# Four 64x64 tiles for a block-of-ones matmul, and an exponential in three parts

## The chip, the cores and the metric

The kernel runs on one core of one Trainium2 chip. The time is that of the device for the whole program, in microseconds: 4799.18 us, the median of three runs (4795.73 to 4809.79).

## The reference

The input is `x` of shape (8, 512, 128), float32. The model has two stages:

```
x = x + attn(layernorm(x))        # 16 heads of 8, causal, weights 1/(lambda - s) with four Newton steps
x = x + ffn(layernorm(x))         # "ffn" is six layers, each: local attention, then a gated MLP
```

One layer of the second stage, for a sequence of 512 tokens and width 128:

```
qkv = shift_tokens(x) @ Wqkv              # 16 heads of 64
q = q / max(norm(q over the head's 64), 1e-12) * q_scale ; the same for k
q, k = rotated (cos, sin, growing and shrinking scale)
attention in windows of 32 tokens, each looking at its own and the window before
x = out @ Wo + x
x = (a * gelu(gate)) @ W2 + b2 + x        # a, gate from layernorm(shift_tokens(x)) @ W1 + b1
```

The change concerns the norms: for every token and head the sum of 64 squares, for q and for k.

## The kernel before, in words

Stage one is untouched. Stage two runs 48 steps, one for each of 6 layers and 8 sequences. In each step the 16 heads are worked in four groups `g` of four heads. Activations lie transposed: partitions are features, columns are the 512 tokens. A projection gives q (or k) of a group as 128 partitions x 2 halves x 512 columns. Partition 32h + i holds feature i of head h, and the second half holds feature 32 + i of the same head.

For one group, the chain is:

- `project` (TensorE) writes q and k into two PSUM banks each.
- `squares` (ScalarE) squares them into `sq`, `rotate` (VectorE) multiplies them by the tables.
- `square_sums` (GpSimd) adds the two halves into `sqs` (128 x 2 x 512, index `which` is 0 for q and 1 for k), `add_rotated` (GpSimd) adds the rotated products.
- `norms` (TensorE) multiplies `sqs` by `ones4`, a 128x128 matrix with ones in its four 32x32 diagonal blocks and zeros elsewhere. So every partition gets its own head's sum. q goes to the first bank, k to the second.
- `log_norms` (ScalarE) takes the logarithm into `lnn`, `inverse_norms` (ScalarE) the exponential of -1/2 of it into `rn`.
- `finish` (VectorE) multiplies `rn` into the rotated q and k.
- `rotated` (SP) sends them with eight DMAs into `qkn`; `scores` (TensorE) reads `qkn`.
- Then `mask`, `row_max` (VectorE), `less_max` (GpSimd), `exponentials` (ScalarE), `denominators` (VectorE), `normalise` (GpSimd), `turn` (TensorE), `turned` (ScalarE), `weigh` (TensorE), `weighted` (VectorE), and for the whole step `out_project`, the layer norm and the MLP.

Every engine has its own `body(b)`, in which the calls for steps b, b-1 and b-2 stand in an order written out by hand. An engine works strictly through this order; semaphores make it wait for others. On TensorE a norms block stands at four places. norm3 (of step b-1) is between `turn` of group 0 and `weigh` of group 0. norm0 is between the two parts of `weigh` of group 1. norm1 is between the first part of `weigh` of group 2 and the first part of `scores` of group 0. norm2 is between the first part of `scores` of group 1 and `values` number 2. PSUM's eight banks are shared by the list `HOLD`; `take` waits until the last holder of a bank was emptied. For instance `mean` takes bank 4 after `values` number 2 (`v2`), which ScalarE copies out.

`scores` and `weigh` already work with small tiles. In `scores` the rows of the array are split in two (the contraction is over 64 partitions) and its columns in four; in `weigh` both are split in two. In both, the two halves of the rows write different PSUM banks. float32 matmuls are recorded as two passes each, with a weight load before each pass.

Of the kernel before, what the change touches and what calls it, by code (L numbers as in the profile page):

```python
# [15 lines left out]
ACT = mybir.ActivationFunctionType  # L16
AX = mybir.AxisListType

P = 128
# [1019 lines left out]
def stage2(nc, consts, wqkv, wod, w1d, w2d, vecd, hist, x1d, out, early):  # L1039
    with ExitStack() as ctx:  # L1040
        def sb(name, shape, dt=F32):
            return ctx.enter_context(nc.sbuf_tensor(name, shape, dt))

        def sem(name):
            return ctx.enter_context(nc.semaphore(name))
# [9 lines left out]
        ones4 = early.ones4  # L1055
# [7 lines left out]
        sqs = sb("sqs", [P, 2, SEQ])  # L1063
        m1 = early.m1
        m2 = early.m2
        lnn = sb("lnn", [P, 2, SEQ])
        rn = sb("rn", [P, 2, SEQ])
# [19 lines left out]
        cst = sb("cst", [P, 4])  # L1087
# [25 lines left out]
        s_rn = sem("s_rn")  # L1113
# [55 lines left out]
        def at(n, k=0, per=NG):  # L1169
            return per * n + (per + k + 1)  # L1170


        def live(b, back):
# [10 lines left out]
        ]  # L1184
        PLACE = {name: i for i, (name, _, _) in enumerate(HOLD)}
        ONE = ("wo", "mean", "var", "gate1", "up1", "out")

# [11 lines left out]


        HELD_LAST = {c: max((back, i) for i, (name, back, _) in enumerate(HOLD) if c in banks(name)) for c in range(8)}
        Y_BANK = [c for c in range(8) if HELD_LAST[c] < (HOLD[PLACE["var"]][1], PLACE["var"])]

# [180 lines left out]
        def _(pe):  # L1384
# [64 lines left out]
            def project(n, g, which, out):  # L1449
# [2 lines left out]
                    mm = pe.matmul(out[:, half, :], wg[:, g, c:c + P], xs[:, 0:SEQ], start=True, stop=True)  # L1452
                mm.then_inc(s_proj[which], 1)

            def norms(n, g, out):
                for which in range(2):
                    mm = pe.matmul(out[:, which, :], ones4[:, :], sqs[:, which, :], start=True, stop=True)  # L1457
                mm.then_inc(s_norm, 1)


# [83 lines left out]
            def body(b):  # L1544
# [30 lines left out]
                if live(b, 1):  # L1575
                    take("norm3", b)
                    squares_due(b - 1, 3)
                    norms(b - 1, 3, bank("norm3"))
# [48 lines left out]
                if live(b, 0):  # L1627
                    take("norm0", b)
                    squares_due(b, 0)
                    norms(b, 0, bank("norm0"))  # L1630
# [29 lines left out]
                if live(b, 0):  # L1660
                    take("norm1", b)
                    squares_due(b, 1)
                    norms(b, 1, bank("norm1"))
# [61 lines left out]
        def _(act):  # L1725
# [12 lines left out]
            def inverse_norms(n, g):  # L1738
                act.wait_ge(s_nf[0], at(n - (g < 1), (g - 1) % NG))
                act.sem_inc(held["act"], 1)  # L1740
                act.wait_ge(s_nf[1], at(n - (g < 1), (g - 1) % NG))
                act.sem_inc(held["act"], 1)
                act.wait_ge(s_lnn, at(n, g))
                nc.scalar.activation(rn[:, :, :], lnn[:, :, :], ACT.Exp, scale=-0.5, bias=cst[:, 2:3]).then_inc(s_rn, 1)

            def values(n, i):
                half, part = i // 2, i % 2
# [47 lines left out]
            def body(b):  # L1795
# [11 lines left out]
                if live(b, 0):  # L1807
                    inverse_norms(b, 0)
# [14 lines left out]
                if live(b, 0):  # L1823
                    inverse_norms(b, 1)
# [10 lines left out]
                if live(b, 0):  # L1835
                    inverse_norms(b, 2)
# [439 lines left out]
```

## Time and profile before

| | |
|---|---|
| median of three runs | 4799.18 us |
| the profiled execution | 4804.87 us |
| its span, first to last instruction | 4803.1 us |
| TensorE (matmul) busy | 4079.8 us, 85% |
| VectorE busy | 3988.7 us, 83% |
| GpSimd busy | 3483.6 us, 73% |
| ScalarE busy | 2994.3 us, 62% |
| norms matmul (line 1457), 768 recorded passes | 383.5 us |
| exponential for `rn` (line 1744), 192 | 1.150 us each |

Shares are averages over both stages; stage two begins at about 1486 us and takes the rest. A matmul's recorded time contains its way through the array, and the next one starts before it ends, so busy times of TensorE overlap. The rows below are of stage two, most of them of one step, and all times in them are in microseconds from the start of the span.

### The profile page before, as it was taken

Reading aid. Unit: us, or ns where it says so; the run is one execution under the profiler, and the core shown is the slowest. Engines: PE = TensorE matmul, PEld = TensorE weight load, DVE = VectorE, ACT = ScalarE, POOL = GpSimd, SP = SyncE. Lnnn points to the kernel's source line nnn. Section 1 sums busy time; section 2 is a strip of 40 time slices with the busy share of each in tenths; the row PEclk is TensorE's granted clock in tenths of the full one; section 3 lists DMA queues with packets and bytes.
Section 4 is the critical chain, followed back from the end, with each engine's and each line's share of the span. In section 5 each row is a group of like instructions: output and inputs, shape, how many; then the busy total and the mean of one; then the engine's idle time right before and its main releaser. Section 6 shows DMA issues by size and latency. Waiting matters only on the chain.

```text
span 4803.1 us, 153853 instructions
## 1 busy us (share of the span) xinstructions
PE 4079.8 (85%) x60260; PEld 2120.9 (44%) x60260; DVE 3988.7 (83%) x7132; ACT 2994.3 (62%) x4240; POOL 3483.6 (73%) x1655
## 2 busy tenths in 40 slices
PE   3666666666656999999999999999999999999997
PEld 1222332233223455555555555555555555555554
DVE  6999999999974788888888888888888888888885
ACT  5999999999983455545555555555555455554552
POOL 4999899999984676667666676666666676666663
PEclk9755555555557999999999999999999999999998
DMA  0000000000003444444444444454444444454443
GB/s 14 3 6 5 10 5 9 5 10 5 3 7 90 103 103 112 118 119 103 105 117 119 114 103 112 118 126 102 103 117 120 114 101 111 118 127 101 104 115 102
DMA packets 230497, 381.82 MB, mean 79 GB/s; under 512 B 38112, under 2 KB 59232, under 8 KB 229728
## 3 DMA queue, kind: packets, MB, share of 16 engines
q1 hardware_dynamic: 229856, 372.57, 32.1%
q8 instruction: 489, 8.01, 0.7%
q14 instruction: 152, 1.25, 0.1%
HBM read 51.57 MB, written 18.61 MB: 15 GB/s over the span
## 4 chain that ended last, share of the span: by engine, by line
PE 46%; issue 6%; DVE 5%; SPq 4%; POOL 3%; DMA 3%; ACT 2%; DVEq 0%; POOLq 0%
PE pb L1452 11%; PE pb L1510 7%; PE pb L1470 6%; PE pb L1493 6%; PE pb L1457 5%; PE pb L1504 4%; PE pb L1521 3%; SPq L1284 3%; PE pb L1533 3%; POOL sqs L1878 3%; DMA qkn<-early 3%; ACT early L1730 2%; PE pb L1480 2%; DVE early L2015 2%; DVE early L1992 1%
## 5 line engine op out<-in xcount | busy, mean ns | idle before, releaser
L783 POOL TENSOR_TENSOR early<-early 128x1280 f32<-128x1280 f32 x416 | 954.9, 2319 | 141.1 <-ACT early L634 139.4
L1878 POOL TENSOR_TENSOR sqs<-early 128x1024 f32<-128x1024 f32 x192 | 468.6, 2441 | 756.5 <-ACT early L1730 756.5
L634 ACT ACTIVATE early<-S,lam 128x512 f32<-128x512 f32 (+3 forms) x2048 | 951.9, 553 | 84.6 <-DVE lam L927 73.2
L1882 POOL TENSOR_TENSOR early<-early 128x1024 f32<-128x1024 f32 x384 | 947.8, 2486 | 19.0 <-DVE early L1992 17.5
L898 DVE BATCH_NORM_STATS2 stats<-early 128x6 f32<-128x512 f32 (+3 forms) x2048 | 832.3, 478 | 57.4 <-POOL early L783 56.2
L1452 PE MATMUL pb<-early 128*128 128x512 f32 x1536 | 734.9, 606 | 2.6 <-POOL early L1955 2.5
L1991 DVE TENSOR_TENSOR early<-pb,early 128x1024 f32<-128x1024 f32 x384 | 467.4, 1217 | 128.1 <-ACT early L1730 115.1
L1730 ACT ACTIVATE early<-pb 128x1024 f32<-128x1024 f32 x384 | 394.0, 1026 | 269.5 <-PE pb L1452 268.9
L2015 DVE SCALAR_TENSOR_TENSOR early<-rn,early 128x1024 f32<-128x1024 f32 x384 | 513.2, 1357 | 54.6 <-POOL early L1882 50.4
L1735 ACT ACTIVATE lnn<-pb,cst 128x1024 f32<-128x1024 f32 x192 | 212.5, 1107 | 492.7 <-PE pb L1457 492.5
L1893 POOL TENSOR_TENSOR pr<-pr,rsum 128x1024 f32<-128x1024 f32 x192 | 365.2, 1902 | 178.7 <-DVE rsum L2028 178.7
L1992 DVE TENSOR_TENSOR early<-pb,early 128x1024 f32<-128x1024 f32 x384 | 465.7, 1213 | 0.0
L1888 POOL TENSOR_TENSOR sm<-sm,mx 128x1024 f32<-128x1024 f32 x192 | 409.2, 2131 | 70.2 <-DVE mx L2006 70.2
L1760 ACT ACTIVATE pr<-sm 128x1024 f32<-128x1024 f32 x192 | 202.2, 1053 | 389.9 <-POOL sm L1888 389.9
L1999 DVE TENSOR_TENSOR sm<-pb,early 128x1024 f32<-128x1024 f32 x192 | 235.0, 1224 | 241.5 <-PE pb L1470 241.4
L1457 PE MATMUL pb<-sqs,early 128*128 128x512 f32 x768 | 383.5, 622 | 32.6 <-POOL sqs L1878 18.6
L1452 PEld LDWEIGHTS pb<-early 128*128 128x128 f32 x1536 | 278.4, 191 | 295.8 <-issue 284.7
L1470 PEld LDWEIGHTS pb<-qkn 64*32 64x32 f32 x24576 | 270.2, 106 | 274.1 <-issue 273.0
L1504 PE MATMUL pb<-early 128*128 128x512 f32 x768 | 367.1, 600 | 1.3 <-ACT lnn L1735 1.3
L1470 PE MATMUL pb<-qkn 64*32 64x64 f32 x24576 | 322.9, 225 | 49.0 <-DVE early L1992 26.1
L423 PE MATMUL psD<-kT,qT 9*128 9x512 f32 (+3 forms) x1024 | 200.3, 741 | 192.5 <-DVE S L889 110.4
L1766 ACT COPY pT<-pb 128x1024 f32<-128x1024 f32 x192 | 194.5, 1013 | 256.9 <-PE pb L1480 256.1
(122 smaller groups left out, 7371.9 us busy)
## 6 DMA issues: line engine op xcount, KB each, us to landing
qkn<-early SPq DMA_DIRECT2D x1536, 128.0 KB, 2.4
vr<-v SPq DMA_DIRECT2D x96, 768.0 KB, 5.8
vr<-v SPq DMA_DIRECT2D x96, 192.0 KB, 5.5
xr<-hist SPq DMA_DIRECT2D x48, 256.0 KB, 4.8
hist<-xo SPq DMA_DIRECT2D x47, 256.0 KB, 4.7
early<-wqkv SPq DMA_DIRECT2D x24, 384.0 KB, 3.5
early<-hist SPq DMA_DIRECT2D x48, 128.0 KB
vr<-v SPq DMA_DIRECT2D x96, 64.0 KB, 6.3
```

Of the source, the lines that this page charges most:

```text
L634: ins = nc.scalar.activation(W[:, p, h, c], S[:, j % 2, h, c], ACT.Abs_reciprocal_sqrt, bias=lam[:, j, i:i + 1])
L783: nc.gpsimd.tensor_tensor(W[:, p, h, :], W[:, p, h, :], W[:, p, h, :], ALU.mult).then_inc(s_wp[p], 1)
L898: ins = nc.vector.bn_stats(out=stats[:, p, h * NBLK + u, :], in_=W[:, p, h, UOFF[u]:UOFF[u] + UNIT[u]])
L1452: mm = pe.matmul(out[:, half, :], wg[:, g, c:c + P], xs[:, 0:SEQ], start=True, stop=True)
L1457: mm = pe.matmul(out[:, which, :], ones4[:, :], sqs[:, which, :], start=True, stop=True)
L1470: mm = pe.matmul(out[o:o + 32, b, (2 * k + s) * 64:(2 * k + s + 1) * 64], qkn[64 * b:64 * b + 64, p, hh, 0, (w + 1) * WIN:(w + 2) * WIN], ...
L1504: mm = pe.matmul(out[:, j, :], xs[:, k * P:(k + 1) * P], wg[:, 2 * half:2 * half + 2, 4 * P:6 * P], start=True, stop=True)
L1730: nc.scalar.activation(sq[:, which, :, :], bank(f"{'qk'[which]}{g}")[:, :, :], ACT.Square)\
L1878: nc.gpsimd.tensor_tensor(sqs[:, :, :], sq[:, :, 0, :], sq[:, :, 1, :], ALU.add).then_inc(s_sqs, 1)
L1882: nc.gpsimd.tensor_tensor(m1[:, which, :, :], m1[:, which, :, :], m2[:, which, ::-1, :], ALU.add)\
L1992: nc.vector.tensor_tensor(m2[:, which, :, :], src[:, :, :], tab[:, which, 1, :, :], ALU.mult)\
L2015: nc.vector.scalar_tensor_tensor(out=nf[:, which, :, :], in0=rn[:, which, :].unsqueeze(1).broadcast_to([P, 2, SEQ]), scalar=1e12, in1=m1[: ...
```

## The change

Each of the two norms matmuls becomes two, of a 64x64 block of `ones4`. The block of ones is block-diagonal, so its off-diagonal 64x64 blocks are zero and are left out. For q the lower half of the partitions goes to the lower half of the output, and the upper to the upper. For k they change places: the lower half of `sqs` is written to partitions 64 to 127 and the upper to 0 to 63. So the four matmuls use the four different 64x64 tiles of the array. q's two write one bank, at different partitions, k's two the other.

`lnn` then holds k's halves swapped. The exponential is done in three instructions: q's whole, and k's two halves, each written to the other half of the partitions.

```diff
             def norms(n, g, out):
                 for which in range(2):
-                    mm = pe.matmul(out[:, which, :], ones4[:, :], sqs[:, which, :], start=True, stop=True)
+                    for half in range(2):
+                        i, o = 64 * half, 64 * (half ^ which)
+                        mm = pe.matmul(out[o:o + 64, which, :], ones4[i:i + 64, i:i + 64], sqs[i:i + 64, which, :],
+                                       start=True, stop=True, tile_position=(i, o))
                 mm.then_inc(s_norm, 1)
...
                 act.wait_ge(s_lnn, at(n, g))
-                nc.scalar.activation(rn[:, :, :], lnn[:, :, :], ACT.Exp, scale=-0.5, bias=cst[:, 2:3]).then_inc(s_rn, 1)
+                nc.scalar.activation(rn[:, 0, :], lnn[:, 0, :], ACT.Exp, scale=-0.5, bias=cst[:, 2:3])
+                nc.scalar.activation(rn[0:64, 1, :], lnn[64:P, 1, :], ACT.Exp, scale=-0.5, bias=cst[64:P, 2:3])
+                nc.scalar.activation(rn[64:P, 1, :], lnn[0:64, 1, :], ACT.Exp, scale=-0.5, bias=cst[0:64, 2:3])\
+                  .then_inc(s_rn, 1)
```

## Rows read from the trace of the kernel before

**Rows 1.** Busy time by engine, 2000:2900: window, length, PE, PEld, DVE, ACT, POOL, clock, DMA share, GB/s.
```profile
2000.00:2900.00 900.00, 869.12 (x15354) 468.27 (x15354) 750.93 (x805) 468.28 (x481) 614.27 (x280) 1.00 0.47 114
```
**Rows 2.** Waits in 2000:2900: waiting line, releaser, total us, times, longest.
```profile
PE pb L1470 <- DMA qkn<-early: 4.4, 12, 0.5
PE pb L1457 <- POOL sqs L1878: 3.5, 14, 0.3
PE pb L1470 <- DVE early L1992: 3.2, 8, 0.4
```
**Rows 3.** TensorE in order of time, one step: start, length, line, tile, count [idle, releaser].
```profile
2433.76 2.31 PE L1452 MATMUL pb<-early 128*128 128x512 f32 x5
...
2440.26 1.98 PE L1457 MATMUL pb<-sqs,early 128*128 128x512 f32 x4
2442.17 0.43 PE L1493 MATMUL pb<-pT,v 64*64 64x32 f32 x16
...
2443.66 0.85 PE L1470 MATMUL pb<-qkn 64*32 64x64 f32 x64 [0.36 <-DMA qkn<-early]
...
2454.61 1.96 PE L1457 MATMUL pb<-sqs,early 128*128 128x512 f32 x4
2457.01 0.85 PE L1470 MATMUL pb<-qkn 64*32 64x64 f32 x64 [0.45 <-DMA qkn<-early]
...
2477.79 1.98 PE L1457 MATMUL pb<-sqs,early 128*128 128x512 f32 x4
2479.61 1.88 PE L1504 MATMUL pb<-early 128*128 128x512 f32 x4
```
**Rows 4.** GpSimd in order of time, the same step.
```profile
2437.20 2.37 POOL L1878 TENSOR_TENSOR sqs<-early 128x1024 f32<-128x1024 f32 x1 [3.90 <-ACT early L1730]
2439.52 1.91 POOL L1888 TENSOR_TENSOR sm<-sm,mx 128x1024 f32<-128x1024 f32 x1
2441.38 4.70 POOL L1882 TENSOR_TENSOR early<-early 128x1024 f32<-128x1024 f32 x2
```
**Rows 5.** VectorE in order of time, the same step.
```profile
2446.11 2.36 DVE L2015 SCALAR_TENSOR_TENSOR early<-rn,early 128x1024 f32<-128x1024 f32 x2 [1.14 <-POOL early L1882]
```
**Rows 6.** SP's DMA issues in order of time, first and last two of eight.
```profile
2448.58 0.59 SPq L1284 DMA_DIRECT2D qkn<-early  x1
...
2453.53 1.25 SPq L1284 DMA_DIRECT2D qkn<-early  x2
```
**Rows 7.** Groups by shape, 2000:2900: line, op, shapes, count, busy us, mean ns, idle.
```profile
L1457 PE MATMUL pb<-sqs,early 128*128 128x512 f32 x216 | 107.0, 618 | 9.2 <-DVE early L1992 5.4 <-POOL sqs L1878 3.5
...
L1744 ACT ACTIVATE rn<-lnn,cst 128x1024 f32<-128x1024 f32 x54 | 62.1, 1150 | 1.8
...
L1760 ACT ACTIVATE pr<-sm 128x1024 f32<-128x1024 f32 x53 | 55.8, 1053 | 108.1 <-POOL sm L1888 108.1
...
L1791 ACT ACTIVATE gl<-pb,vec 128x512 f32<-128x512 f32 x26 | 16.4, 684 | 0.2
```
**Rows 8.** TensorE, matmuls started in 2409.72:2409.80 (scores) and 2425.1:2425.2 (weigh).
```profile
2409.75 0.28 PE L1470 MATMUL pb<-qkn 64*32 64x64 f32 x7
...
2425.16 0.26 PE L1493 MATMUL pb<-pT,v 64*64 64x32 f32 x4
```
**Rows 9.** TensorE in order of time around norm3, and the mean of the next step.
```profile
2423.27 1.95 PE L1457 MATMUL pb<-sqs,early 128*128 128x512 f32 x4 [0.24 <-POOL sqs L1878]
2425.16 0.43 PE L1493 MATMUL pb<-pT,v 64*64 64x32 f32 x16
...
2484.03 1.02 PE L1514 MATMUL pb<-xm,early 128*128 128x512 f32 x2
```
**Rows 10.** ScalarE in order of time: pT's copy before weigh0, `rn`, v2's copy.
```profile
2423.10 1.02 ACT L1766 COPY pT<-pb 128x1024 f32<-128x1024 f32 x1
...
2443.56 1.15 ACT L1744 ACTIVATE rn<-lnn,cst 128x1024 f32<-128x1024 f32 x1
...
2482.02 0.99 ACT L1753 COPY v<-pb 128x1024 f32<-128x1024 f32 x1
```

## The prediction

> **What bounds the kernel now.** I read first which engine has least idle time in the second stage (where the change is), then what TensorE waits for, then its order of time beside the other engines. In 900 us of that stage TensorE is busy 869 us at a granted clock of 1.00, VectorE 751, GpSimd 614, ScalarE 468 [rows 1]. So TensorE is the nearest bound, and at first sight every microsecond taken from it is won. The waits say where it is not: the scores wait for the DMA that brings qkn and for VectorE's rotation, the norms for GpSimd's sum of squares, each time by tenths of a us [rows 2]. Such small waits on the busiest engine mean a second chain that is just as long. I follow one step (one sequence in one layer) in order of time.
>
> The long chain: k0's projection ends at 2433.76 + 2.31 = 2436.07 [rows 3]. ScalarE squares it, and then GpSimd works without a gap: squares' sum from 2437.20 (its row says it idled 3.90 us until ScalarE), a subtraction for group 2, two sums of rotated halves, done at 2446.08 [rows 4]. VectorE's two `finish` follow, 2446.11 to 2448.47 [rows 5]. SP issues the eight transfers of `rotated`, the first at 2448.58, the last ending at 2454.78 [rows 6], and group 0's scores start at 2457.01 after a wait of 0.45 for the landing [rows 3]. That is 20.94 us, and the norms matmul is nowhere in it: the chain meets it only if `rn` comes after GpSimd's 2446.08. In the same 20.94 us TensorE runs norm0 and norm1 and has waits left over. From score0 to the next k0 I find no such chain; TensorE is back to back except for norm3's wait.
>
> **Part 1: the four tiles.** Before, a block is two matmuls, recorded as four passes over 512 columns. Passes start 0.43 us apart ((1.88 - 0.59) / 3 from the row of values at 2479.61 [rows 3]; a single one is recorded with about 0.6 [rows 7]), so 1.72 us, and in place 1.82 to 1.91, the rest being changes between 128x128 and small tiles. After, it is four matmuls, eight passes of the same 512 columns, on four different tiles. Do tiles run side by side in this type? Seven passes of the scores start in the first 0.05 us [rows 8], though each streams 64 columns, which at 0.43 us for 512 takes 0.054; and four passes of `weigh`, in the same four 64x64 tiles as the new norms, start within 0.04 us [rows 8]. If that holds, four first passes start together, four second ones 0.43 later: the block occupies the array 2 x 0.43 + 0.03 = 0.89 us. Below this the least is 0.43 (both passes of a tile at once, as no row excludes strictly); above, 8 x 0.43 = 3.44 (nothing beside anything). I take 0.89, since `weigh` is the same tile form.
>
> One thing has no row: here both row halves write one PSUM bank, at different partitions, at the same time. In `scores` and `weigh` each row half has its own bank. If the hardware made them take turns, the block would cost 1.72 as before. The Trainium skill ("TensorEngine Tiling (Array Packing)", Restrictions and Gotchas) states that different row tiles cannot access the same PSUM bank simultaneously; by that rule the block stays at 1.72. Its page "PSUM — Partial Sum Buffer" (bank collisions) puts the conflict per bank and group of 32 partitions, and no two tiles here share those. No row of this trace decides between them.
>
> **What each block gives.**
> - norm2: from 2477.79 to values at 2479.61 is 1.82 [rows 3]. After, 0.89, and the change to 128x128 (0.10) now falls before `values`: gain 0.83.
> - norm3: 2423.27 to 2425.16 is 1.89 [rows 9]. After, `weigh` could start at 2424.16, in the same mode. It needs pT, whose copy ends at 2424.12 [rows 10], so it just gets it: gain 0.95, and no more even if the block were free.
> - norm0: 2440.26 to 2442.17 is 1.91, norm1 about the same [rows 3]. Both shrink by about 1.0 with no mode change left between them and `weigh`. Both lie between k0 and score0, so they only lengthen waits: score3's 0.36 becomes about 1.4, score0's 0.45 about 2.5. Gain 0.
>
> **Part 2: three exponentials for one.** One over 1024 columns takes 1.150, against 1.053 without a bias operand; activations of 512 columns with a bias take 0.684 each [rows 7]. Three make 3 x 0.684 = 2.05, so about +0.85 us. A floor is 1.15 (no fewer columns pass), a ceiling 3 x 1.15 = 3.45, if partitions that are shifted by 64, which no row shows, cost as much as the whole. I take 2.0, by the rows of that size. What hides the 0.85: for norm1 to norm3, the logarithm starts when the norms end, 0.9 earlier, so `rn` is ready when it was. For norm0 the logarithm waits for an exponential of group 2 instead, so `rn` is late by the 0.85: ready at 2444.71 + 0.85 = 2445.56 [rows 10], still before GpSimd's 2446.08. Behind norm2, ScalarE's queue holds the copy of v2, which frees `mean`'s bank. It ended at 2483.01 [rows 10], with `mean` at 2484.03 [rows 9]; now 2482.95 against 2483.2, 0.25 to spare. Without this cover each further 0.1 costs 0.1.
>
> **The sum.** 0.83 + 0.95 = 1.78 us a step; 47 steps follow the first: 84 us, less 2 for the ends, where blocks don't follow closely. The profiled execution took 4804.87 us (span 4803.1), so 4723; the median of the runs is 5.7 below it: **4717 us**, its own range 4705 to 4735. What is late next is score0, by the transfers, with the norms' part of TensorE's time cut in half and only 45% of the cut paid out.
>
> **Rivals.**
> - *All of it is paid out.* The waits of 0.45 are small, and an earlier finish elsewhere might bring transfers forward. Then 3.8 us a step, 47 x 3.8 = 179: 4620. Against it, GpSimd has no gap between 2437.20 and 2446.08.
> - *The block is nearly free* (0.43): norm2 gives 1.3, norm3 still 0.95, 47 x 2.25 = 106: 4693.
> - *Another wait takes half*: the bank for `mean` with 0.25 in hand, or pT for weigh0. 47 x 0.9 = 42: 4757.
> - *Turns at the bank, no gain*: block 1.72, exponentials 0.85 later: the copy of v2 then ends at 2483.86, still ahead of 2484.03. About 4797. The change would do nothing it says.
> - *Slower, by order.* If passes start strictly in program order, a tile's second pass waits 0.43 for its first and holds back the next tile: first passes at 0, 0.43, 0.86, 1.29, the last second pass ending at 2.15. norm2 +0.43, norm3 +0.26, norm0 and norm1 hidden: 47 x 0.69 = +32: 4831. With nothing overlapping (3.44): +1.72, +1.55, and 3.06 less the waits of 0.36 and 0.45: 5.5 a step, 5058. It decides from a block over about 1.85 us. Against it: seven starts in 0.05 us in [rows 8], where in strict order the second pass would be 0.054 behind the first. The Trainium skill ("TensorE: Matmul & The Clock Gate", Part 3) says that matmuls start and end in strict program order; by it this rival's 4831 is the forecast. The trace speaks against it.
> - *Slower, by ScalarE.* Exponentials of 3.45: norm0's `rn` comes at 2447.01, 0.90 behind GpSimd; `mean` is 1.2 late. 2.1 lost against 1.78 won: 47 x 0.3 = +15: 4814. It decides from about 3.2 us for the three.
>
> **How the numbers follow.** The forecast 0.66, all paid out 0.03, nearly free 0.04, half 0.09, turns at the bank 0.08, slower 0.10 (order 0.07, ScalarE 0.03). A difference of under 0.3% (14 us) can't be told from none here; so faster 0.82, same 0.08, slower 0.10. Range 4690 to 4790: it takes in the forecast, half and nearly free, 0.79.
>
> **What would show it.** Records of the norms: eight passes, starts in two clusters 0.43 apart, last end about 1.05 after the first start (strict order: the last pass starts at 1.7; turns at the bank: at 1.3). The three exponentials 1.9 to 2.1 together. Group 0's scores waiting 2 to 2.5 us for DMA or VectorE's rotation in each step, group 3's about 1.4. norm3's wait for GpSimd still there. VectorE's share up to 85%, TensorE's idle time up despite the shorter time. I am wrong if score0's wait stays below 1 us, if `finish` begins to wait for ScalarE's `rn`, or if norm passes keep 0.43 between starts throughout.

## The result and the profile after

The changed kernel takes 5045.3 us (median of 4 runs, 5042.9 to 5057.7), the kernel before 4804.5 beside it: ratio 1.051, interval 1.048 to 1.053. Forecast were 4717 us and a range of 4690 to 4790. The change made the kernel slower and not faster.

The page of the changed kernel: span, busy time by engine, and from its part on DMA queues (packets, MB, share) the queue that brings TensorE's instructions.

```profile
span 5044.9 us, 155773 instructions
...
PE 4054.5 (80%) x61028; PEld 2079.9 (41%) x61028; DVE 4033.4 (80%) x7132; ACT 3192.8 (63%) x4624; POOL 3426.6 (68%) x1655
...
q8 instruction: 490, 8.03, 0.7%
```

Busy time by engine in the same 900 us of stage two; it answers to [rows 1]. The clock is now 0.96 on average, and every engine but ScalarE does less work in the same time:

```profile
2000.00:2900.00 900.00, 798.55 (x14378) 422.45 (x14381) 702.34 (x739) 475.08 (x532) 551.64 (x257) 0.96 0.43 104
```

What TensorE waits for in those 900 us (waiting line, releaser, total us, times, longest), against [rows 2]:

```profile
PE pb L1498 <- issue: 37.1, 34, 2.7
PE pb L1452 <- issue: 20.6, 12, 2.7
PE pb L1475 <- DVE early L2000: 13.3, 12, 1.3
PE pb L1452 <- ACT v L1761: 12.2, 11, 1.3
```

The first two lines are as good as new (before, `weigh` waited 0.5 us for "issue" and the projections never), and they are the result: 58 us in which TensorE waited for nothing that the profile shows, in `weigh` (1498) and in projections (1452). The third is score0's wait, grown as forecast, and the fourth a wait of k1 for ScalarE that I had not seen coming.

TensorE in order of time, pieces of one step, to be held against [rows 3]: score0; the end of `weigh` of group 2 (weigh2) behind its stop, and FFN's output; norm2 and `values`; norm3; k0 in two parts; the second part of weigh1; k1.

```profile
2434.28 0.85 PE L1475 MATMUL pb<-qkn 64*32 64x64 f32 x64 [1.28 <-DVE early L2000]
...
2437.95 0.43 PE L1498 MATMUL pb<-pT,vr 64*64 64x32 f32 x6 [1.78 <-issue]
2438.68 5.02 PE L1538 MATMUL pb<-gl,w 128*128 128x512 f32 x6 [0.30 <-issue]
...
2459.07 1.09 PE L1461 MATMUL pb<-sqs,early 64*64 64x512 f32 x8
2460.09 1.99 PE L1509 MATMUL pb<-early 128*128 128x512 f32 x4
...
2471.46 1.09 PE L1461 MATMUL pb<-sqs,early 64*64 64x512 f32 x8 [0.25 <-POOL sqs L1886]
...
2480.07 1.88 PE L1452 MATMUL pb<-early 128*128 128x512 f32 x4
2484.11 3.65 PE L1452 MATMUL pb<-early 128*128 128x512 f32 x4 [2.16 <-issue]
...
2493.78 0.37 PE L1498 MATMUL pb<-pT,v 64*64 64x32 f32 x11 [0.67 <-issue]
...
2498.63 1.96 PE L1452 MATMUL pb<-early 128*128 128x512 f32 x4 [1.30 <-ACT v L1761]
```

See three things. The block of norms is eight passes in 1.09 us, as forecast, and `values` starts 1.02 us behind its start instead of 1.82. In the middle of k0 and of `weigh`, between two matmuls of one function, TensorE stands for 2.16 and 1.78 us for "issue". And behind these two stops the matmuls are twice as long: FFN's output takes 5.02 us in place of 1.52 + 1.45 for its six passes, the second half of k0 3.65 in place of 1.8. The granted clock behind the stop in weigh2 is one level down, 1.2 GHz (0.50, first row); the stretch from there to k0's stop is back at 2.4 GHz (1.00, second row):

```profile
2436.40:2443.10 6.70, 4.85 (x12) 2.14 (x12) 3.73 (x4) 1.51 (x3) 4.20 (x2) 0.50 0.01 2
2443.20:2484.00 40.80, 37.92 (x666) 19.31 (x664) 32.55 (x35) 23.99 (x27) 23.29 (x11) 1.00 0.51 124
```

The slow clock is not behind every stop. Over 44 steps of the loop it follows the stop in weigh2 in 43 and the one in weigh1 in none. It follows the one in k0 in only 6, and there the stop is longer than in the others (2.8 against 2.1 us from one instruction's start to the next). The k0 shown above is one of the six.

**Where the stops are.** I number TensorE's recorded instructions from the branch back of its loop (one turn is one step) and take the median time from the start of each to the start of the next over the loop's 40-odd steps. Before, a turn has 2411 instructions and no stop over 0.7 us. After, it has 2443 (in each of four norms blocks four more passes and their four weight loads), and the long ones are always at the same three numbers, 781, 1037 and 1805: each is 13 more than a multiple of 256. A packet on queue 8 carries 8.03 MB / 490 = 16.4 KB, and there are ten in a turn, one for each 256 instructions or part of it. So TensorE runs to the end of the instructions that it has, and the next block isn't there. For the 2.16 us stop above, which is longer than most at this place, what the DMA engines did in the 1.36 us up to the stop and during it:

```profile
q1 hardware_dynamic: 128, 0.20, 79.6%
...
q1 hardware_dynamic: 12, 0.01, 2.7%
q8 instruction: 1, 0.02, 2.7%
```

First data alone; the instruction packet comes when that ends. Times of the packets by the same count, in us behind the branch back (medians):

```
                          packet 1   packet 2          packet 3   packet 6
before: start to landing  15.5-16.6  21.6-22.8         29.4-30.6  47.3-48.4
        block needed at   19.2       24.1 (781)        31.9       49.3 (1805)
after:  start to landing  15.0-16.0  21.5-22.8         29.7-31.1  48.9-50.1
        block needed at   18.3       21.9, goes on     31.2, on   49.5, on
                                     at 24.1           at 32.5    at 51.5
```

TensorE goes on 1.35 to 1.4 us behind a landing (medians at each of the three stops). Before, 781 is reached at 24.1, just as packet 2 becomes usable. Norm3's eight more instructions move the boundary eight instructions towards the front, and norm3 and weigh0 are done 0.9 earlier; so the boundary is reached at 21.9, with the packet where it was.

**The account of a step** (medians, on TensorE, after less before; period 67.0 before, 72.3 after): norms blocks -3.5 (four of 0.87); stall in k0 +1.8; stall in weigh1 +1.1; in weigh2 +2.0; FFN's output at half clock +1.5; k1's wait for v0's copy +1.2; score0's wait +0.9; weigh0's start +0.4; mean +0.3; turn1's and score3's waits -0.6 and -0.3. That is +4.8 of 5.3; the rest is in small waits.

### The profile page after: what moved, and what is told of

The parts are those of the page before. It is cut to its first block, busy times and chain, and to the rows that moved or that the text cites. A ratio compares the mean times of both kernels' runs of the same rounds, so it can differ in the third digit from the quotient of the medians.

```text
span 5044.9 us, 155773 instructions
## 1 busy us (share of the span) xinstructions
PE 4054.5 (80%) x61028; PEld 2079.9 (41%) x61028; DVE 4033.4 (80%) x7132; ACT 3192.8 (63%) x4624; POOL 3426.6 (68%) x1655
## 3 DMA queue, kind: packets, MB, share of 16 engines
q8 instruction: 490, 8.03, 0.7%
## 4 chain that ended last, share of the span: by engine, by line
PE 44%; issue 9%; POOL 6%; ACT 6%; DVE 3%; SPq 1%; DMA 1%; ACTq 0%; POOLq 0%; DVEq 0%
PE pb L1452 14%; PE pb L1515 6%; PE pb L1475 5%; PE pb L1498 5%; PE pb L1538 4%; POOL sqs L1886 4%; PE pb L1526 4%; ACT early L1735 3%; PE pb L1509 2%; PE pb L1461 2%; DVE early L2000 2%; POOL sm L1896 2%; DVE early L1999 1%; PE pb L1485 1%; ACT lnn L1740 1%
## 5 line engine op out<-in xcount | busy, mean ns | idle before, releaser
L1886 POOL TENSOR_TENSOR sqs<-early 128x1024 f32<-128x1024 f32 x192 | 456.2, 2376 | 837.4 <-ACT early L1735 837.4
L1890 POOL TENSOR_TENSOR early<-early 128x1024 f32<-128x1024 f32 x384 | 903.1, 2369 | 19.1 <-DVE early L2000 17.5
L1452 PE MATMUL pb<-early 128*128 128x512 f32 x1536 | 758.6, 618 | 122.6 <-issue 71.8
L2023 DVE SCALAR_TENSOR_TENSOR early<-rn,early 128x1024 f32<-128x1024 f32 x384 | 551.4, 1457 | 60.6 <-POOL early L1890 53.4
L1498 PE MATMUL pb<-pT,vr 64*64 64x32 f32 x12288 | 349.1, 221 | 81.7 <-issue 81.7
L1498 PE MATMUL pb<-pT,v 64*64 64x32 f32 x12288 | 342.2, 221 | 58.5 <-issue 54.0
L1509 PE MATMUL pb<-early 128*128 128x512 f32 x768 | 375.1, 611 | 3.8 <-ACT lnn L1740 2.3
```

What stands on the lines that cost most here:

```text
L1498: mm = pe.matmul(out[64 * b:64 * b + 64, s, o:o + WIN], src[64 * s:64 * s + 64, k, c:c + DH2], pT[64 * s:64 * s + 64, b, r:r + WIN], start ...
L1886: nc.gpsimd.tensor_tensor(sqs[:, :, :], sq[:, :, 0, :], sq[:, :, 1, :], ALU.add).then_inc(s_sqs, 1)
L1890: nc.gpsimd.tensor_tensor(m1[:, which, :, :], m1[:, which, :, :], m2[:, which, ::-1, :], ALU.add)\
L2023: nc.vector.scalar_tensor_tensor(out=nf[:, which, :, :], in0=rn[:, which, :].unsqueeze(1).broadcast_to([P, 2, SEQ]), scalar=1e12, in1=m1[: ...
```

## Experiments

Ratios are to the kernel before on the same chip. "Stop at n" is the n-th instruction of the turn, in medians over steps. The theory (F): boundaries of instruction blocks and late packets cost the time. Its rivals: (S) ScalarE's exponentials do, (T) the tiles themselves do.

**The change taken apart.** e1 keeps the tiles and puts one exponential back; the keys' norms are then swapped. e2 keeps the old norms and takes three exponentials, in place. e3 has the old 128x128 matmul in two halves of columns: as many passes as after (eight), but no tile and no gain. e4 has the old matmul over 256 of 512 columns, each sum used twice, so that half of the sums are left out: a short block with the old number of instructions.

```diff
 e1
-  nc.scalar.activation(rn[:, 0, :], ...); rn[0:64, 1] ; rn[64:P, 1]
+  nc.scalar.activation(rn[:, :, :], lnn[:, :, :], ACT.Exp, scale=-0.5, bias=cst[:, 2:3])
 e3
-  mm = pe.matmul(out[:, which, :], ones4[:, :], sqs[:, which, :], ...)
+  for c in (slice(0, 256), slice(256, SEQ)):
+      mm = pe.matmul(out[:, which, c], ones4[:, :], sqs[:, which, c], ...)
 e4
+  mm = pe.matmul(out[:, which, 0:256], ones4[:, :], sqs[:, which, 0:256], ...)
```

> The change without its ScalarE half: four tiles, but one exponential over all of lnn, so that the keys' halves stay swapped (leaves the putting back out). The changed kernel's TensorE stands still for 1.5 to 2.3 us at three places of each step (k0, weigh of group 1, weigh of group 2), each at an instruction that lies 256 behind the last such one, with nothing waited for; instruction packets on their own DMA queue are 16 KB. Theory F (instruction packets come late): these stalls have nothing to do with ScalarE and stay; only k1's wait for v0's copy (1.0 us) and score0's (part of 1.3 us) go. Time 4950 to 5010. Theory S (ScalarE's longer exponentials set off the rest): stalls and slow clock go, 4710 to 4760.

> Only the three exponentials, each half read and written in place; norms as before. Theory F: no new stall at 256-instruction places; k1 waits 0.3 to 0.5 us for v0's copy and mean perhaps 0.2 for v2's, so 4805 to 4840. Theory S: most of the 241 us, 4950 or more.

> Norms as before in 128x128, but each in two column halves of 256: eight passes as in the change (32 instructions more in a step), array time as before, one exponential. Theory F1 (it is where the packet boundaries fall): a stall of over 1 us at k0 and perhaps in weigh of group 2, 4850 to 4950. Theory F2 (it is how fast TensorE eats its instructions because the norms are shorter): no stalls beyond those of before, 4800 to 4820. Theory S: 4800 to 4820.

> Norms in 128x128 over the first 256 columns only, the logarithm reads these twice (the other half's sums are left out): the block takes 0.9 us as in the change, the instruction count and packet boundaries are those of before, one exponential. Theory F1: no stalls, the gain that was forecast: 4710 to 4740. Theory F2: stalls in weigh of group 1 and 2, 4800 or more. Theory S: 4710 to 4740.

Measured: e1 1.039 (1.037 to 1.041), e2 1.009 (1.008 to 1.011), e3 1.036 (1.034 to 1.038), e4 0.998 (0.996 to 0.999). e1 (4990 us) is inside what F expected. e2 (4848) is 8 us above F's range, e3 (4981) 31 above F1's. e4 (4794) missed F1's 4710 to 4740.

e3 is the one to look at. It neither shortens the norms (a block takes 1.89 us in place of 1.88) nor touches ScalarE; its first two waits:

```profile
PE pb L1494 <- issue: 23.3, 14, 2.1
PE pb L1452 <- issue: 13.0, 11, 1.7
```

Its boundaries are 20 more than a multiple of 256, and so are its stops, at 788 (1.74 us) and 1812 (2.00). So 32 more instructions a step cost 3.6% alone. There is no small tile in it, so (T) isn't needed. e1 has the changed kernel's three stops and most of its loss. e2 has no long stop, only k1 waiting for v0's copy (9 times, up to 0.7 us; in the median step k1 starts 0.44 late) and `mean`, which starts 0.33 late: (S) is real and is 0.9%, about 45 us. e1 and e2 together, 4.8%, make nearly the whole 5.1%.

e4 shows what is left of the forecast gain without more instructions: 0.2%. In the median step norm2's part is paid, and no more: the period is 66.15 us in place of 67.01. norm3's is lost in the next wait of `turn1` (0.97 in place of 0.51), norm0's in a stop of 0.78 at 1036, norm1's in score0's wait of 1.26. The first is a wait for VectorE, and it stands in the trace before too (waits in 2000:2900, before and then e4):

```profile
PE pb L1480 <- DVE gl L2074: 5.6, 12, 1.0
```

```profile
PE pb L1480 <- DVE gl L2075: 11.1, 12, 1.0
```

That 0.86 us a step would be 40 us. The median of ten runs gained 10, and the profiled one, among the slowest, nothing (4803.7 us). In 11 of its 45 steps some passes, in FFN's output or from `values` to k1, start 0.85 us apart, the distance at half clock. These steps take 67.4 to 68.4 us, together some 20 us more than at the others' pace, though no stop in them is over 1.4 us. The second stage has about 180 us at half clock in place of 70.

**Moving the boundaries.** The loop's head can be laid at another place of its block; nothing else changes. e5 and e6 did this with the changed kernel, e7 has the four tiles and three exponentials for groups 2 and 3 only, e8 the same with another place.

```diff
-  head_slot={mybir.EngineType.PE: 0}) as b:
+  head_slot={mybir.EngineType.PE: 64}) as b:     # e5; e6: 224; e8: 208
 e7, e8
+  if g < 2:   # the matmul and the exponential of before
```

> The changed kernel, with the head of TensorE's loop placed at instruction 64 of a fetch block of 256 instead of 0 (head_slot); nothing that is computed or issued is different. From the changed kernel's trace, without its stalls, TensorE would then use up two of its ten blocks in 2.5 us each, and one in 3.7 (now the shortest are 3.7, 4.1 and 4.7 us, and behind the 3.7 and 4.1 stand the long stalls). Theory F1 (block boundaries decide): more or longer stalls, at other instructions, each 256 apart again: 5060 to 5200. Theory not-F (stalls hang on what TensorE does there, on the clock or on the tiles): the same places, 5045.

> The changed kernel with the loop head at instruction 224 of a block. The shortest blocks would be 4.2, 4.2, 4.4 and 4.6 us. Theory F1: k0's and weigh2's long stalls shrink to under 1 us each, the half-speed stretches of the clock behind them go, k1's wait for ScalarE stays: 4850 to 4960. Theory not-F: 5045.

> Four tiles and three exponentials for groups 2 and 3 only, groups 0 and 1 as before; loop head at 0. These two are the blocks from which I had forecast the gain. k1's wait for v0's copy doesn't arise. 16 instructions more in a step than before, 8 of them ahead of k0. Theory F1: boundary 3 of the loop moves from the semaphore waits before turn1 toward k0: a stall of about 1 us there, less than in the change at weigh2: 4800 to 4900. Without any fetch trouble it would be 4720.

> As groups 2 and 3 only, with the loop head at instruction 208 of a block, where by the trace of the kernel before the shortest blocks are 4.4 to 4.5 us instead of 3.6. Theory F1: fewer stalls than with the head at 0, 4740 to 4800, perhaps faster than the kernel before. Theory not-F: as the one with the head at 0.

Measured: e5 1.062 (1.060 to 1.065), e6 1.057 (1.054 to 1.059), e7 1.022 (1.019 to 1.026), e8 1.054 (1.052 to 1.056). e5 is in its expected range, e7 (4908 us) 8 us above its own. e7 adds 16 instructions and not 32, and keeps the stops at 781 (2.0) and 1805 (1.7). In the other three the stops moved with the boundaries: e5 to 461 (2.30) and 2253 (1.41), both 205 more than a multiple of 256, which is 13 - 64. But no place was better. e6 and e8 missed what I had expected: 781 and 1805 were free of stops, and a new one of 4.0 to 4.2 us came right behind the branch back, at 44 and 60. e6's and e8's first rows:

```profile
PE pb L1475 <- issue: 51.2, 15, 5.5
```

```profile
PE pb L1476 <- issue: 48.9, 20, 5.1
```

**One group only.** Group 2's norms are the last thing in the turn, so their eight more instructions move no boundary of it but the first.

```diff
+  if g != 2:   # the matmul and the exponential of before
```

> Four tiles and three exponentials for group 2 only. Its block is the last of TensorE's step, behind nine of the ten block boundaries of the loop, so the 8 more instructions move none of those that matter. Theory F1: no new stalls, and norm2's share of the forecast is paid out, as it was with half the columns: 0.8 us a step, 4755 to 4775. Theory T (the tiles or the exponentials themselves cost the time): slower than the kernel before, 4830 or more.

Measured: 4784.7 us, 0.9966 (0.9955 to 0.9978) over 7 runs. No stop over 0.63, a period of 66.6. It beats both kernels, by 17 us, where I had expected 26 to 46: the step gained 0.4 us and not the 0.8 by which the block is shorter. The trace has the other 0.4: score1 and k3 start 0.78 earlier than before, `mean` behind them only 0.50 and the projection after it 0.42. `mean` waits for v2's copy, which stands behind the three exponentials.

**The data ahead of the packet.** e10 to e12 move the copies of v to vr behind the transfers of `rotated(b - 1, 3)` in SP's order, on e7, on the kernel before and on e9.

```diff
-  rolled(b - 1, 1)
   rotated(b - 1, 3)
+  rolled(b - 1, 1)
```

> Groups 2 and 3 as above (4908), and SP issues the three vr transfers of the second half (1 MB) after group 3's qkn transfers instead of before. The packet that k0 waits for starts 2.9 us after its block was free, in the middle of the vr traffic, others about 1 us after. Theory D (data transfers delay instruction packets): that packet starts 1 to 2 us earlier, k0's stall of 2.3 shrinks below 1, another may grow: 4840 to 4890. Theory L (the delay is a fixed latency of the fetch): unchanged, 4895 to 4925.

> The kernel before with only SP's order changed in the same way, as the control: theory D and L 4780 to 4810.

> Group 2 only, with SP's order changed. Theory D: turn1's wait shrinks too, down to what VectorE's gate sets, 4740 to 4770; theory L: as group 2 alone.

Measured: e10 1.039 (1.037 to 1.041), e11 1.015 (1.014 to 1.017), e12 1.012 (1.010 to 1.013). Packet 2 starts 2.0 to 2.4 us earlier, and e7's stop at 781 is gone in e10 (the one at 1805 stays). But packet 4 came 2.4 to 2.6 later, behind the moved data, with a new stop of 1.5 us at 1293 or 1294 in all three. All three missed what was expected. e11 is the kernel before with this one edit; there this wait was 0.6 us in 900 before, and is now:

```profile
PE pb L1470 <- issue: 18.0, 22, 1.7
```

**Boundaries alone.** I chose places so that no block of 256 is over in less than 4.1 us: 104 and 96 for the changed kernel, 96 for the unchanged one. 128 tests the branch back.

> The changed kernel whole, with the head of TensorE's loop at place 104 of its block of 256 instructions instead of 0. All that it computes stays. Laid over the changed kernel's own times, every block boundary then closes a block that TensorE needs at least 4.1 us for, a short block always has one of 8 us or more beside it, and the first boundary lies 5 us or more behind the loop's branch. Theory (where the boundaries fall, not the change's own work, costs the time): the waits for issue of over 1 us in the k0, weigh1 and weigh2 blocks go, and ffn_out runs at full clock again; from the step of 72.3 us that takes 1.62 + 1.1 + 2.0 + 1.5 and gives back 0.7 at the first turn, so about 66.8 us: 4790 us, range 4740 to 4860. Rival (the change costs as such: more instructions, small tiles, three exponentials, wherever the boundaries fall): 4980 or more.

> The same with the head at place 96: shortest block 4.1 us, first boundary 8 us behind the branch. Theory: as with 104, 4740 to 4860, no issue wait over 1 us at a fixed place. Rival: 4980 or more.

> The kernel before, its instructions unchanged in number and order, with the head of TensorE's loop at place 96. Theory: boundaries alone move. All blocks last 4.2 us or more but one towards the step's end that lasts 2.8 behind one of 6.6, so one stall of up to 1.5 us a step there at most: 4800 to 4880 us. If it costs nothing, below 4800. Rival (the boundaries don't matter by themselves): 4801 within 0.3%.

> The changed kernel with the head at place 128: the blocks are as good as with 104 in the middle of the step, but the first boundary follows 3.1 us behind the branch back, where places 208 and 224 had a stall of 3.2 to 3.4 us behind 2.6 us. Theory with the limit at the branch: a stall of about 2.9 us at the 141st instruction, with half clock behind it: 4950 to 5080. Theory without that limit (places 208 and 224 were slow for another reason): 4740 to 4860, as with 104.

Measured: e13 1.072 (1.070 to 1.074), e14 1.074 (1.072 to 1.076), e15 1.066 (1.064 to 1.068), e16 1.084 (1.080 to 1.087). My rule of the block's length was not enough: all four are slower than its ranges, e15 by 240 us. e13's stops are at 421, 677 and 2213 (2.0, 1.1, 1.65 us), each 165 more than a multiple of 256, which is 13 - 104 + 256. But e15 is the cleanest evidence of all: the same 2411 instructions in the same order, 316 us slower. TensorE in order of time in e15:

```profile
2417.38 0.29 PE L1493 MATMUL pb<-pT,v 64*64 64x32 f32 x7
2418.79 0.32 PE L1493 MATMUL pb<-pT,v 64*64 64x32 f32 x9 [1.12 <-issue]
...
2422.15 1.14 PE L1470 MATMUL pb<-qkn 64*32 64x64 f32 x93
2425.80 0.85 PE L1470 MATMUL pb<-qkn 64*32 64x64 f32 x35 [2.51 <-issue]
```

Its stops are at 430, 686 and 2222 (1.62, 2.46, 1.50 us), each 174 more than a multiple of 256, which is 14 - 96 + 256. The last is the short block that was expected to cost up to 1.5 us: its packet starts at 60.2, 1.6 us after TensorE has entered the block before, with no data ahead, and that block lasts 2.8. The first two have no short block, but data: packet 1 starts at 14.8 us, at the end of a stretch that has the DMA engines at a share of 0.9 from 10.5 us on, packet 2 at 22.0, at the end of the next (0.9 to 1.0 from 18 on), though TensorE had entered the block before at 8.5 and 17.4. The DMA engines' share in the microsecond before a packet's start is 0.9 to 1.04 for both of them. In e16, the stop behind the branch back came (2.3 us at 141, and 4.3 in front of its prefetch hint at 13), larger together than the 2.9 expected; there packet 1 starts at 6.9, and the burst of vr's first half lasts until 6.5.

**The data taken away.** One of v's four blocks is copied instead of all.

```diff
-  sp.dma_start(vr[0:P - WIN, :, c], v[WIN:P, :, c])
+  sp.dma_start(vr[0:P - WIN, 0:1, c], v[WIN:P, 0:1, c])
-  sp.dma_start(vr[P - WIN:P, 0:NBLK - 1, c], v[0:WIN, 1:NBLK, c])
+  sp.dma_start(vr[P - WIN:P, 0:1, c], v[0:WIN, 1:2, c])
```

> The changed kernel, but only one of v's four blocks is copied to vr (a quarter of these transfers' bytes; the rest of vr is zero). In the changed kernel TensorE's third instruction packet of a step starts 3.2 us after TensorE has entered the block before, with the DMA engines full in the microsecond ahead (share 0.99) by vr's second half, and it lands 0.85 us after TensorE has run dry in k0. Theory (the packet waits behind vr's data): the packet starts by 19.5 to 20 instead of 21.5 us after the loop's branch, the stall at the 781st instruction goes, and with its part of the slow clock 1.6 us of 72.3 a step: 4970 us, range 4900 to 5010. The stalls at 1037 (its packet waits behind the transfers of rotated halves, which stay) and at 1805 (no data ahead of its packet) stay. Rival (the packet is late by itself, or the transfers cost elsewhere): the stall stays at 1.5 us or more, 5030 or more.

> The kernel before, with the same quarter of the copies to vr. Theory: the same packet starts earlier here too, but there TensorE loses only 0.2 to 0.7 us at this boundary, so little changes: 4770 to 4805 us. Rival (the copies cost time in themselves, by traffic or by SP's issues): it falls by as much as the changed kernel does.

Measured: e17 4998.5 us, 1.040 (1.037 to 1.042); e18 1.000 (0.999 to 1.001). In e17 packet 2 starts at 18.9 in place of 21.5 and the stop at 781 is gone; k0 runs through in 3.60 us, and the wait behind it is the ordinary one:

```profile
2479.51 3.60 PE L1452 MATMUL pb<-early 128*128 128x512 f32 x8
2484.09 1.06 PE L1485 MATMUL pb<-early,pr 128*128 128x128 f32 x8 [0.99 <-DVE gl L2082]
```

1037 (1.1) and 1805 (1.8) kept theirs, as expected. The gain of 47 us is inside the range but less than the 75 forecast: part of the 2.2 us came back as turn1's wait, and the second stage has some 370 us at half clock in place of 290. The same cut on the unchanged kernel brings packet 2 from 21.6 to 19.5 and no time. So in the kernel before the data cost nothing, and in the changed one they cost through the packet that must get past them.

## Why the prediction was wrong

- **The block: right.** Forecast were 0.89 on the array and a last end 1.05 behind the first start; measured 1.09, and 0.87 gained in each of the four. The eight passes start in two clusters, four within 0.02 us and four 0.48 later. Two matmuls that write one bank at different partitions don't take turns. So the rule of the Trainium skill ("TensorEngine Tiling (Array Packing)", Restrictions and Gotchas) that different row tiles cannot access one PSUM bank at once is not borne out for different partitions. The Trainium skill's page "PSUM — Partial Sum Buffer" (PSUM bank collisions), by which the conflict is one of bank and group of 32 partitions, fits. The rival made from strict order (the Trainium skill, "TensorE: Matmul & The Clock Gate", Part 3) did not come: it would have made 2.15. That does not speak against the page's rule itself, since the records don't tell which matmul a pass belongs to, and their starts and ends are in order.
- **The exponentials: 2.0 forecast, 2.19 measured** (three of 0.72, 0.73 to 0.74 from start to start). The cover was mis-stated. `mean`'s bank, with 0.25 in hand, came 0.28 late: 0.19 is the exponentials' excess, and 0.30 passes between the end of v2's copy and the start of `mean` (e9: 2400.95 and 2401.25), a term that the prediction put at nothing. And I looked at v2's copy alone: v0's copy stands behind the same exponentials, and frees the banks for k1, with 0.66 to 0.79 in hand by my reading of the trace since. ScalarE of the changed kernel in order of time:

```profile
2494.13 1.10 ACT L1740 ACTIVATE lnn<-pb,cst 128x1024 f32<-128x1024 f32 x1
2495.26 0.72 ACT L1749 ACTIVATE rn<-lnn,cst 128x512 f32<-128x512 f32 x1
2496.00 0.72 ACT L1750 ACTIVATE rn<-lnn,cst 64x512 f32<-64x512 f32 x1
2496.73 0.72 ACT L1751 ACTIVATE rn<-lnn,cst 64x512 f32<-64x512 f32 x1
2497.47 1.93 ACT L1761 COPY v<-pb 128x1024 f32<-128x1024 f32 x2
```

  k1 starts at 2498.63, in the midst of these two copies, and later than its data. The late k1 also makes group 1's rotation on VectorE late, and score0 with it: from k1 to score0 it is 10.7 us before and 10.8 after. This miss is 0.9% (e2), half as large as the gain forecast, and would have been visible in the trace before.
- **The chain from k0 to score0: right in what it costs, wrong in its last link.** From turn1 to score0 it is 20.65 us before and in e4, though both blocks between them are shorter there: gain 0, as forecast. But score0 starts 0.41 us behind the end of VectorE's rotation of group 1, before, in e4 and after alike (medians over the steps). The last transfer for it has landed 0.85 us ahead of score0 before, and 1.2 in the other two. score0's wait became 1.28 and not 2 to 2.5. The forecast had counted norm0's 1.0 twice, once in score3's wait and again in score0's: 0.45 and norm1's 0.87 make 1.3.
- **The sum, "norm2 0.83 and norm3 0.95": the step that failed**, with the sentence that it rests on: "From score0 to the next k0 I find no such chain; TensorE is back to back except for norm3's wait". The first half of what went wrong is a wait between engines. turn1 stands right behind k0 and already waited 0.42 us there for VectorE, the largest sum in the list of TensorE's waits (5.6 us in 900), which [rows 2] leaves out. e4 turns norm3's gain into that wait: in its median step 0.86 us are gained, norm2's, and not 1.78. So the forecast was twice too high even without a stop. The second half made the kernel slower, and it is not between engines: TensorE's own instructions. The forecast counted time on the array and no instructions. It had 16 more passes and 16 more loads a step, 32 in 2411, and a queue of instruction packets on the page that I didn't read. The boundary at 781 had been reached just when its packet was there (24.1 against 22.8 + 1.35). The change took 0.9 us away in front of it and moved it forward, and three boundaries became stops of 2.2, 1.2 and 2.0 us, with the clock at half behind the last of them in nearly every step.
- **What would have shown it.** Of the marks set, score0 under 1 us, `finish` waiting for `rn` and 0.43 between all starts, none occurred, and the forecast still fell: none of them looked at "issue". In the trace before, L1480 had one wait of 1.4 us for issue in 900 us, and the count from the loop's branch would have put a boundary 0.2 us from a stop.

The Trainium skill knows the mechanism ("Runtime: NRT & Kernel Launch", Instruction fetch mechanics): blocks of 16 KiB, 256 instructions, fetched over the sequencer's own DMA queue while the one before runs. This trace agrees with the size. It calls the cost of crossing a boundary "mostly hidden"; here it is hidden before and 1.2 to 2.2 us at three of ten boundaries after.

**What stays open.** When exactly a packet is asked for: some start 0.8 to 1.1 us after TensorE has entered the block before, with the DMA engines idle; e15's packet 1 did not start in 1.5 idle microseconds, and the one for 1805 comes 3.4 us later with no data ahead of it. How the cost divides between stops and slow clock: e15 has some 260 us at half clock and takes 5120 us, e17 370 and takes 4998. And what four tiles in all groups would give with no boundary in a bad place: none of six places tried was good, so it was not seen. By the pieces that were measured it would be well under the forecast: norm3's part goes to turn1 (e4), 0.4 us of norm2's to `mean` (e9), and k1 waits for v0's copy on top (0.4 in e2, 1.2 after).

## What to carry to other kernels

Where an engine runs hundreds of small instructions in a few microseconds, count an edit's instructions as well as its time: look at the waits for "issue", number the instructions from the loop's branch, and see how far each 256th is from the landing of its packet and which data stand ahead of it. Work that is shortened ahead of such a point can gain nothing, and added instructions can cost more than they save, unless they move no boundary (here at the turn's end, e9, 0.3% faster). And of each instruction made longer, ask what every copy queued behind it frees, not only the nearest.

## What the runs showed of the hardware

- The same instructions in the same order took 4803 and 5120 us by where in its block of 256 the loop begins (e15, 6.6%).
- Instruction packets of 16.4 KB share the DMA engines with data and wait behind a burst: packet 2 starts at 21.5 us in the changed kernel and at 18.9 with a quarter of the bytes ahead (e17). From landing to the next instruction it takes 1.35 to 1.4 us.
- A stop of about 2 us in TensorE can be followed by work at 1.2 GHz, passes 0.85 us apart for 3 to 5 us, and need not be. After: in 43 of 44 steps behind the stop at 1805, in 6 behind the one at 781, in none behind 1037 (1.2 us). e3: in 23 of 45 behind 1812 (2.0 us), in none behind 788 (1.7 us). The second stage had about 70 us at half clock before, 290 after, 60 in e9.
- Four 64x64 tiles in float32 run side by side, two writing one bank: four matmuls of 512 columns in 1.09 us, against 1.98 for two of 128x128.
- ScalarE writes to partitions 64 away from those it reads at no price: 718 and 720 ns for 64 shifted partitions, 722 for 128 straight ones, in the groups by shape of the changed kernel (count, busy us, mean ns, idle):

```profile
L1749 ACT ACTIVATE rn<-lnn,cst 128x512 f32<-128x512 f32 x48 | 34.7, 722 | 1.6
L1751 ACT ACTIVATE rn<-lnn,cst 64x512 f32<-64x512 f32 x48 | 34.6, 720 | 0.6
L1750 ACT ACTIVATE rn<-lnn,cst 64x512 f32<-64x512 f32 x48 | 34.5, 718 | 0.6
```
